# A four-layer attention block: another opening, another buffer for the keys' parts, and units of the next batch element in other places

## What is computed

```python
# layer 0: 16 heads of 64, softmax over the QUERIES (axis 2)
A = where(mask == 0, -inf, q @ k.T / 8);  alpha = softmax(A, axis=2)
x = (alpha @ v) @ W_O.T + b_O + x
# layer 1: gated fusion with the mean of the context
vision_proj = mean(ctx) @ Wv.T + bv;  agreement = sum(text_proj * vision_proj)
gate = sigmoid(text_proj @ Wg_t.T + (r * vision_proj) @ Wg_v.T + bg)   # r: softmax of 2 * agreement
x = layernorm(x + gate * r * vision_proj)
# layer 2: relu'd q, k, v, 16 heads of 16, causal, keys masked; normalize
# layer 3: banded self-attention (64 keys back, per-head slopes), layernorm,
#          full cross-attention, layernorm, feed-forward 256 -> 1024 -> 256 (gelu), layernorm
```

## Time and profile before

| | us |
|---|---|
| median of 3 runs (range) | 1961.23 (1958.24 to 1963.94) |
| profiled execution, its own time | 1963.6 |
| its span in the trace | 1961.8 |
| FIRST, from the start to about | 125 |
| loop rounds, from about | 125, 605, 1076 |
| LAST, from about | 1543 |

### The profile page before, as it was taken

How to read it: one execution, slowest core, us unless ns; L and a number is a source line. 1 busy time by engine, 2 the same in 40 slices (tenths; PEclk the granted TensorE clock), 3 DMA queues, 4 the chain that set the end, 5 groups by cost and what they waited for, 6 DMA issues and landing times.

```text
span 1961.8 us, 25180 instructions
## 1 busy us (share of the span) xinstructions
PE 1576.9 (80%) x8920; PEld 812.5 (41%) x8920; DVE 926.9 (47%) x2240; ACT 725.8 (37%) x1281; POOL 250.2 (13%) x121
## 2 busy tenths in 40 slices
PE   7999878887887878687886987879688877757676
PEld 3245434442255534344234643444223654445234
DVE  4643554456712465455751256454672255333641
ACT  2632452433720244353551135434364024222342
POOL 4001002020022001102013000201102210202001
PEclk9998888887998899889798989988889867767688
DMA  6012202213012310403121140130401040131110
GB/s 250 22 65 65 44 1 66 43 33 76 22 65 71 75 34 21 83 7 87 21 86 42 47 91 1 40 63 7 107 22 65 11 89 3 39 54 33 33 44 11
DMA packets 43445, 99.95 MB, mean 51 GB/s; under 512 B 10929, under 2 KB 21297, under 8 KB 41009
## 3 DMA queue, kind: packets, MB, share of 16 engines
q1 hardware_dynamic: 37840, 86.02, 17.6%
q10 hardware_dynamic: 5472, 12.22, 2.1%
HBM read 58.36 MB, written 2.10 MB: 31 GB/s over the span
## 4 chain that ended last, share of the span: by engine, by line
PE 49%; DVE 19%; issue 15%; ACT 7%; SPq 7%; DMA 1%; DVEq 0%; POOLq 0%; POOL 0%; ACTq 0%
PE ring L1328 7%; DVE nmax L1122 7%; PE ring L1349 6%; SPq L504 4%; PE ring L1550 4%; PE obank L1508 4%; PE ring L1489 4%; PE ring L1273 3%; PE obank L1308 3%; PE ring L1285 3%; PE ring L1458 2%; PE ring L1297 2%; SPq L511 2%; ACT q_all L830 2%; PE ring L1340 2%
## 5 line engine op out<-in xcount | busy, mean ns | idle before, releaser
L1122 DVE TENSOR_REDUCE nmax<-ring 128x2 f32<-128x1024 f32 (+4 forms) x384 | 309.8, 853 | 211.8 <-PE ring L1458 153.4
L839 ACT ACTIVATE region_e<-ring 128x1024 f32<-128x1024 f32 (+4 forms) x384 | 270.3, 731 | 345.5 <-PE ring L1458 221.4
L967 DVE CUSTOM_DVE_ANT_0 region<-ring,maskb 128x512 f32<-128x512 f32 x256 | 165.8, 686 | 187.4 <-issue 187.3
L1508 PE MATMUL obank<-region_e,region_v 128*32 128x512 f32 (+4 forms) x1536 | 171.8, 533 | 35.7 <-DVE region_qt L1148 35.7
L743 ACT ACTIVATE region<-region,nmin 128x512 f32<-128x512 f32 x256 | 181.7, 714 | 14.9 <-DVE nmin L967 14.6
L1308 PE MATMUL obank<-region,vs 128*64 128x512 f32 x512 | 153.6, 681 | 35.8 <-DVE v L957 35.0
L1458 PE MATMUL ring<-cbf 64*128 64x128 bf16 (+1 forms) x2048 | 180.7, 265 | 0.0
L1297 PE MATMUL ring<-qk 64*128 64x512 f32 x512 | 158.1, 702 | 26.9 <-ACT q_all L830 14.4
L1472 PE MATMUL ring<-k_tiles_a,q_all 64*128 64x512 f32 (+4 forms) x384 | 98.8, 529 | 65.8 <-DMA q_all<-q_parts 33.6
L622 POOL TENSOR_TENSOR q_all<-zero 128x1024 fp32r<-128x1024 f32 x32 | 60.4, 1900 | 651.5 <-PE ring L1458 316.3
L1489 PE MATMUL ring<-q_all,k_tiles_a 64*128 64x512 f32 (+4 forms) x384 | 88.0, 464 | 52.1 <-ACT region_e L839 41.0
(11 more groups left out here) (158 smaller groups left out, 2241.2 us busy)
## 6 DMA issues: line engine op xcount, KB each, us to landing
q_all<-q_parts SPq DMA_DIRECT2D x288, 64.0 KB, 2.3
k_tiles_a<-k_parts SPq DMA_DIRECT2D x144, 64.0 KB, 2.8
k_tiles_b<-k_parts SPq DMA_DIRECT2D x144, 64.0 KB, 2.3
wqk<-in_wqk ACTq DMA_DIRECT2D x34, 256.0 KB, 2.7
region_k<-in_w_f SPq DMA_DIRECT2D x8, 1024.0 KB, 5.0
stage_b<-in_stage_l SPq DMA_DIRECT2D x4, 1280.0 KB, 5.5
stage_a<-in_stage_ls SPq DMA_DIRECT2D x4, 1280.0 KB, 6.6
stage_b<-in_stage_lc SPq DMA_DIRECT2D x4, 1280.0 KB, 5.5
```

The costliest lines, as they stand in the source:

```text
L839: act.activation(e16[:, n % E16, 2 * u:2 * u + 2, 0:nq], slot((a, "B", g, kt, u))[:, :, 0:nq], ACT.Exp)\
L967: ins = dve.tensor_tensor_reduce(out=e0[:, n % E0, h, :], in0=slot(name)[:, h, :], in1=maskb[:, :], scale=-1.0, scalar=3.0e38, op0=ALU.add ...
L1122: dve.tensor_reduce(nmax[:, qt, 2 * u:2 * u + 2], slot(name)[:, :, 0:nk], AX.X, ALU.max, negate=True)\
L1508: ins = pe.matmul(obank[32 * s:32 * s + 32, 1, q0:q0 + nq], v_h[:, kt, h, :], e16[:, n % E16, s, 0:nq], start=(kt == 0), stop=(kt == NT - ...
```

## The change

- **Opening.** `vp`, `vpT` and `uv` move: PE now starts a round with O0, then K2, `vp`, the values, X 0, `vpT`, V2, `uv`. DVE sums the context behind its two drains of O0, and ACT copies `vpT` behind X 0.
- **Keys' parts.** `k_parts` now lies in the third exponential unit, `v2` and `w_om` in the second. ACT's wait for the stacks of groups 1 to 3 moves from unit 0 to unit 2 of group 0, and in BANDED SP issues k1, q1, k2, k3, q2, q3. `load_om` is issued behind F2.
- **Queries' parts.** For BANDED and FULL ACT makes the high part straight from PSUM with the bias, and DVE the low part in one operation for each half; before, DVE wrote the full value, ACT copied it, and DVE subtracted.
- **First product of a pair** (`values0` of a unit with n % 4 = 0) goes into the step behind, ahead of the next one.
- **Other places for units.** The U at kt = 3 moves to kt = 2 ahead of V, the U of group 0 ahead of the two A, and CAUSAL's last group has no U.
- **`keep_warm`.** Where no first attention is woven in (LAST), each call of `weave.keys()` makes PE compute 12 products of 128x512 bf16 that nobody reads. There are nine calls in LAST.

```diff
-STEPS_AT = {CAUSAL: ((1, 3), (1, 3), (1, 3), (1,)), BANDED: ((1, 3),) * GROUPS, FULL: ((1, 3),) * GROUPS}
+STEPS_AT = {CAUSAL: ((1, 2), (1, 2), (1, 2), ()), BANDED: ((1, 2),) * GROUPS, FULL: ((1, 2),) * GROUPS}
...
-        steps += [("K", 1), ("T", 0)] + ahead[:2] + [("U", 1)]
+        steps += [("K", 1), ("T", 0), ("U", 1)] + ahead[:2]
...
+        if kt == 2 and kt in STEPS_AT[a][g]:
+            steps.append(("U", 1))
         if n >= 2:
             steps.append(("V",) + divmod(n - 2, NT))
-        if kt in STEPS_AT[a][g]:
+        if kt == 1 and kt in STEPS_AT[a][g]:
             steps.append(("U", 1))
...
     def keys(self, n=1):
+        if not self.on:
+            self.idle(12)
...
-        k_parts = overlay("k_parts", at_e + 4 * 2048, [P, 2, DT, S])
-        v2 = region_e[:, 4096:5120].rearrange("p (t n) -> p t n", t=NT)
+        k_parts = overlay("k_parts", at_e + 4 * 4096, [P, 2, DT, S])
+        v2 = region_e[:, 2048:3072].rearrange("p (t n) -> p t n", t=NT)
...
-                for g in range(1, GROUPS):
+                if a == BANDED:
+                    stack_k(1, k_high + k_low)
+                stack_q(1, q_high + q_low)
+                for g in range(2, GROUPS):
                     if a == BANDED:
                         stack_k(g, k_high + k_low)
+                for g in range(2, GROUPS):
                     stack_q(g, q_high + q_low)
...
-                        act.activation(q_parts[:, 0, t, :], q_full[:, t, :], ACT.Copy).then_inc(q_hi_ready, 1)
+                        if n:
+                            act.wait_ge(*((q_half, b * 3 + n + 1) if t == 0 else job.filled_by(name)))
+                            act.activation(q_parts[:, 0, t, :], slot(name)[:, t, :], ACT.Identity, bias=col(bias, t)).then_inc(q_hi_ready, 1)
+                            continue
...
-                                if g == 0 and which == [0, 0, 0]:
+                                if which == [0, 2, 0]:
                                     for k in range(1, GROUPS):
                                         act.wait_ge(k_stacked[k], (b * 3 + a + 1) * 96)
...
+                        dve.wait_ge(q_hi_ready, (b * 3 + n) * DT + t + 1)
+                        ins = dve.scalar_tensor_tensor(out=q_parts[:, 1, t, :], in0=slot(name)[:, t, :], scalar=col(bias, t),
+                                                       in1=q_parts[:, 0, t, :], op0=ALU.add, op1=ALU.subtract)
...
-                    if 3 <= n < UNITS0 + 3:
+                    if n >= 4 and (n - 4) % NT == 0:
+                        values0(n - 4)
+                    if 3 <= n < UNITS0 + 3 and (n - 3) % NT:
                         values0(n - 3)
...
+                        pe.matmul(obank[:, 0, :], cb("ident", P), cb("keyrows", S), start=True, stop=True)
```

86 lines of the change are left out of this document (46 added, 40 removed).

## The result

The changed kernel takes 1933.45 us (median of 4 runs, 1930.18 to 1939.04), the kernel before 1959.74 in the same comparison (4 runs): a ratio of 0.9876, 95% interval 0.9851 to 0.9900, so 26 us less. The forecast was 1883, with a range of 1862 to 1920. Faster was right; two thirds of the gain are missing.

A forecast was written before the change was run, and what follows sets the result against it. PE was taken as nearest its limit, bounded by its idle places and the clock behind them; 25.6 + 41.2 + 3 - 2.1 + 11.7 - 9.9 + 9 = 78.5 us gave 1883 us, range 1862 to 1920.

The forecast's parts named there:

- opening: Top of rounds and LAST: O0 starts earlier, 2.0 us in round one, 8.8 in two and three, 6 in LAST; 25.6.
- keys' parts: BANDED's group 0: the wait for the keys' stacks goes, 10.8 us a round and 8.8 in LAST; 41.2 together.
- queries' parts: FULL's queries: the path loses DVE's write of 0.75 us each time; nothing in BANDED; 3 us in all.
- idle products: LAST: keep_warm's products let turns and the work behind run at full clock; +9 us, ends -8 and +14.
- groups: Attention groups, walked one by one: CAUSAL 0.5 lost, BANDED 2.4 won, FULL 2.6 lost a round; -2.1 us in all.
- outside: Behind O2 the turn comes 2.5 us earlier, behind OS the wait of 1.35 goes; 3.9 a round, 11.7 in all.
- unit 31 behind the norm: Ahead of the feed-forward: scaling, a cold product and the turn follow the norm, 3.3 us later; -9.9 in three rounds.
- First products and other places: Pairs' first products and moved steps: -2.1 us inside the groups, 11.7 gained outside them.
- the step's 2.1 us come back: Third CAUSAL group: against 3.6 us of waiting at kt = 2, V no longer waits and the step's 2.1 us return.
- rival (4): Slower: the kt = 2 step's slot costs 6.1 us at each of 27 places, 165 in all, giving 2046 us; chance 0.03.
- The forecast's own sign of being wrong: First O0 product 10 us behind F2, or kt = 2 scores waiting over 4 us in most groups.
- The 3.3 us for PE's entry: Top of a round: PE needs 3.3 us after F2 before O0 starts, taken from DVE's 3.12 us without a releaser.

The follow-up runs named there:

- 1853.9: The kernel of 1849.5 with the queries' parts of BANDED and FULL made as in the kernel before: 1853.92 us, ratio 0.9484 to the kernel before.
- 1849.5: Changed kernel with all second steps at kt = 3 behind V, and unit 31 scaled ahead of the norm in DVE's list: 1849.48 us, ratio 0.9449.
- 1876.5: The kernel of 1856.0 with the first product of a pair in its own step again: 1876.48 us, ratio 0.9591 to the kernel before.
- 1856.0: Changed kernel with second steps at kt = 3 behind V and a first step in CAUSAL's last group; group 0's step stays moved: 1856.01 us, ratio 0.9485.
- 1893.1: The kernel of 1856.0 with group 0's step behind the two A again: 1893.11 us, ratio 0.9684 to the kernel before.
- 1922.5: Changed kernel with one step more in CAUSAL's last group (at kt = 1), so unit 31 is scaled ahead of the norm: 1922.55 us, ratio 0.9835.
- 1916.4: Changed kernel with unit 31 scaled ahead of the residual and norm in DVE's list alone: 1916.35 us, ratio 0.9779.
- the old table: The kernel before's table of steps' places (second step at kt = 3, a step in CAUSAL's last group), put into the changed kernel: 1856.01 us.

## Why the prediction was wrong

| term | forecast | runs | from |
|---|---|---|---|
| opening | 25.6 | 37 | 1921.2, alone |
| keys' parts | 41.2 | 22 | 1935.8, alone |
| queries' parts | 3 | 4, unclear | 1853.9 against 1849.5 |
| idle products | 9 | 14 | 1942.9, alone |
| first products | in "groups" and "outside" | 20 | 1876.5 against 1856.0 |
| group 0's step | none | 37 | 1893.1 against 1856.0 |
| second step at kt = 2 | in "groups", -2.1 | -66.5 | 1922.5 against 1856.0 |
| unit 31 behind the norm | -9.9 | -17 | 1933.5 against 1916.4 |

The terms don't add: the six gains sum to 134, while all of them together, with the old table, give 102. They were measured on different kernels, and where one wait goes another can stand behind it.

**The term that failed** is "First products and other places", the groups' -2.1. The walk did find the slot that the step at kt = 2 needs, and DVE's head_out ahead of it. For the third CAUSAL group it gave 3.6 us of waiting, and 3.46 were measured; over the eight places of round two it is 2.0 on average (5.07 at most), so the wait was not underrated. What failed is what was set against it: "the step's 2.1 us come back", V's saved wait, 2.4 won in BANDED. The step's time doesn't come back, since V, B, T, B, V are done behind the wait and no longer beside DVE's head_out and minima; by an estimate from the forecast's own figure that is 24 x 2.1 = 50 of the 66.5 us. What V saves is real but small (its waits for head_out are 25 us in nine attentions of the run of 1856 us, against some 65 that the steps wait for minima with kt = 2). And the products behind the waits, "PE cold behind it", got no number: 13 of 61 us by the profiles.

The rival (4) named this slot and 27 such places, with 2.5 us of cold work behind each and nothing given back, and got 0.03, because groups 0 have no head_out and V's old wait of 1.99 was smaller. Neither made it rare. There are 24 such places (CAUSAL's last group has no second step), 66.5 us are 2.8 for each, and from 78.5 / 24 = 3.3 on the kernel would have been slower. The rival was treated as all or nothing, and two fifths of it (66.5 of 165) belonged in the sum. Its price for a place was too high, its mechanism right: taking head_out out of the wait gave back 59. The forecast's own sign of being wrong, waits of over 4 us in most groups, did not come; one place in a round has that. The loss was larger than the waits, which are 50 us in the changed kernel's nine attentions.

**Outside the groups** 11.7 were forecast, 2.5 a round behind O2 and 1.4 behind OS. From O2 to BANDED's first pass A 1.0, 0.9 and 2.3 us were won, and from KC to FULL's 0.1 to 0.2: some 5 in all.

**Group 0** has no term at all, though the diff moves its step: T's copies were priced at the groups' seams only, and the earlier trace rows shows the 1.61 us of waiting for `q_all` that the move fills. It made up for 37 us of the failure above, so that the total is nearer to the forecast than its terms are: that is luck.

**Unit 31:** the step was right (projection to F1 3.3 longer) and its size off: 5.5. Missing was POOL's pass at the same moment, which makes the scaling 2.46 in place of 0.29: 3.3 + 2.2 = 5.5.

**The opening:** right in order and cause. The 3.3 us for PE's entry are zero at this place: O0 follows F2 without a gap. O0 also met no half-speed time (14.08, not 16.3). Part of both was given back behind K2. By the run with the opening alone, up to CAUSAL's first pass A, 3.0 us were won in round one (forecast 2.0), 10.8 and 10.9 in two and three (8.8), and 11.1 in LAST (6): half of the 11 us more are LAST's. In the changed kernel K2 of round one starts 5 us earlier (134.5 against 139.8), but only 2.5 of that are the opening's (137.3 with it alone); the rest is the first products' in FIRST (137.5 in the run without their shift).

The prediction cites the Trainium skill, "Runtime: NRT & Kernel Launch", section "Instruction fetch mechanics": a taken branch whose target isn't in the pages already fetched forces a fetch before work goes on. At the branch itself PE shows no such stall. But the waits without a releaser behind `vp`, 1.17 and 1.95 us, stand some 20 us behind the branch, only in the two rounds that it leads back into. Whether they are such fetches no run here shows.

**Keys' parts:** the mechanism is right in each detail that the profile can show (0.55 in place of 6.77, 1.65 at unit 2 in LAST). LAST won 10.0 us for the 8.8 forecast, but the rounds 8.0, 9.8 and 4.5 for 10.8 each. That price was taken from round two, which has the longest of the three waits (round one's is 3.50). In the run with the keys' parts alone PE's busy time in BANDED fell by 5.3 and 3.8 us in rounds one and two and rose by 1.7 in round three, where the wait of 6.27 went all the same: the half-speed time that was to vanish with the wait did so twice of three times. So the stages won 32 in place of 41. That the kernel won 22 is in part CAUSAL's other speed in round three, and for the rest stays open.

**Behind OS** the forecast's 1.4 a round is won in front of QC and lost behind it: FULL's first pass A waits for SP. SP loads the next weights over OS's operand `stage_a`, which it can only when OS ends, and then needs 7.5 + 7.6 us for the keys' stacks ahead of the first query. Pass A starts 21.8 us behind the projection's end before and 21.6 after.

## What to carry to other kernels

When a piece of work moves on one engine, walk the list of the engine that answers it: what stands ahead of the answer there, and what of the first engine's work used to run in that time. A wait that is predicted on the path is a loss until a row shows what runs beside it; "something else gets its time back" is not that. Give the slower work behind the wait a number too: here it was a fifth to a half of the loss. And read every round's row before a price from one of them is multiplied. A drain that frees nothing urgent belongs behind the answer for which another engine stands still; where its own reader is next, as V is with the old places, the same drain belongs ahead of it.
